# Head by head instead of with zeros: exact attention scores from stacked rounded parts, on one core

## What is computed

```
q = (xq @ Wq + bq).reshape(B, Lq, 16, 8)
k = (xk @ Wk + bk).reshape(B, Lk, 16, 8)
scores = einsum('bqhd,bkhd->bhqk', q, k) / sqrt(8)
out = einsum('bhqk,bkhd->bqhd', softmax(scores), v)
x = x + out.reshape(B, Lq, 128) @ Wo + bo
```

## Time and profile before

| | us |
|---|---|
| median of 3 runs | 1052.72 (1051.87 to 1052.78) |
| span of the profiled execution, first to last instruction | 1049.9 |
| TensorE matmuls busy | 1008.1 |
| TensorE weight loads busy | 636.9 |
| VectorE busy | 748.8 |
| GpSimd busy | 686.9 |
| ScalarE busy | 607.4 |

### The profile page before, as it was taken

One profiled execution on the slowest core, in us unless ns is written; L12 is line 12 of the kernel. 1 busy time (PEld: TensorE's weight loads), 2 busy tenths in 40 slices (PEclk: granted clock), 3 DMA queues, 4 the chain that ended last, 5 costly groups with the idle time before them and its releaser, 6 DMA issues.

```text
span 1049.9 us, 28844 instructions
## 1 busy us (share of the span) xinstructions
PE 1008.1 (96%) x11729; PEld 636.9 (61%) x11729; DVE 748.8 (71%) x1852; ACT 607.4 (58%) x898; POOL 686.9 (65%) x819
## 2 busy tenths in 40 slices
PE   7889999999999999999999999999999999999998
PEld 5345555556655776667676655665556566565576
DVE  7778888778884443776787788878888866777421
ACT  2144445577667455455554576776666677766752
POOL 6688988687986332111114699987889777688720
PEclk9699999999999999999999999999999999999999
DMA  6300000000001102000000000000000000000011
GB/s 217 122 2 2 22 12 13 20 14 23 12 22 28 36 31 99 13 7 7 8 7 19 14 8 2 2 2 2 3 1 2 2 2 2 2 2 2 1 41 41
DMA packets 9282, 22.76 MB, mean 22 GB/s; under 512 B 1392, under 2 KB 1648, under 8 KB 8768
## 3 DMA queue, kind: packets, MB, share of 16 engines
q1 hardware_dynamic: 9152, 20.94, 5.9%
HBM read 18.77 MB, written 2.15 MB: 20 GB/s over the span
## 4 chain that ended last, share of the span: by engine, by line
PE 82%; DVE 7%; POOL 5%; issue 4%; ACT 2%; DMA 0%; SPq 0%; POOLq 0%; ACTq 0%; DVEq 0%
PE weighed L708 12%; PE scores L680 11%; PE row_scores L643 7%; PE scores L906 6%; PE weighed L731 5%; PE scores L598 4%; PE quads L579 4%; DVE negmax L1226 3%; PE quads L605 3%; PE scores L693 3%; PE row_scores L906 3%; PE quads L590 3%; PE row_scores L721 2%; PE scores L721 2%; PE weighed L923 2%
## 5 line engine op out<-in xcount | busy, mean ns | idle before, releaser
L1226 DVE TENSOR_REDUCE negmax<-row_scores 128x8 f32<-128x616 f32 (+1 forms) x312 | 298.8, 958 | 100.4 <-PE row_scores L643 74.9
L1731 ACT ACTIVATE p<-scores 128x1024 f32<-128x1024 f32 (+1 forms) x253 | 250.9, 1020 | 165.6 <-PE scores L693 139.2
L680 PE MATMUL scores<-qblk,work 32*77 32x512 f32 (+1 forms) x1256 | 202.8, 612 | 6.2 <-ACT p L1731 3.3
L708 PE MATMUL weighed<-p,v 77*32 77x128 f32 (+1 forms) x5120 | 172.9, 276 | 0.1
L1906 POOL TENSOR_TENSOR qblk<-work,pack_const 128x512 f32<-128x512 f32 x160 | 166.5, 1041 | 0.0
L1916 POOL TENSOR_TENSOR kblk_r<-work,pack_const 128x308 fp32r<-128x308 f32 (+1 forms) x160 | 134.0, 838 | 44.4 <-PE row_scores L643 27.0
L643 PE MATMUL row_scores<-kblk_r,qr 32*128 32x308 f32 (+1 forms) x624 | 140.9, 443 | 13.8 <-DVE negmax L1226 12.3
L708 PEld LDWEIGHTS weighed<-p,v 77*32 77x32 f32 (+1 forms) x5120 | 130.0, 109 | 36.0 <-issue 29.4
L643 PEld LDWEIGHTS row_scores<-kblk_r,qr 32*128 32x128 f32 x624 | 61.4, 185 | 98.0 <-issue 70.9
L693 PE MATMUL scores<-nblk,select 32*77 32x512 bf16 (+1 forms) x628 | 94.8, 376 | 0.0
L1242 DVE STREAM_TRANSPOSE nat<-weighed 128x256 f32<-128x256 f32 x160 | 70.9, 443 | 32.6 <-PE weighed L708 30.7
(11 more groups left out here) (332 smaller groups left out, 1862.9 us busy)
## 6 DMA issues: line engine op xcount, KB each, us to landing
shared<-gates_hbm SPq DMA_DIRECT2D x24, 256.0 KB, 3.1
shared<-in_ctx_tok SPq DMA_DIRECT2D x15, 154.0 KB
pack_w_l<-in_w_l SPq DMA_DIRECT2D x1, 2058.5 KB, 11.5
x<-in_x_tok SPq DMA_DIRECT2D x8, 256.0 KB, 6.2
out_x<-x SPq DMA_DIRECT2D x8, 256.0 KB, 2.0
layers_w<-in_w_l SPq DMA_DIRECT2D x1, 1289.0 KB, 9.8
ctxT<-in_ctxT SPq DMA_DIRECT2D x1, 1232.0 KB, 8.9
layers_w<-in_w_ada SPq DMA_DIRECT2D x1, 582.0 KB, 5.5
```

The source lines that it names most:

```text
L680: mm = e.matmul(score_banks(n, g // 2)[0:nk, g % 2, :], k_of[q % 3][at, s * nk:(s + 1) * nk], qblk[n % 2][at, :], start=layer.mask != "qk" ...
L708: mm = e.matmul(av_bank[TILE * j:TILE * j + TILE, i2 * S:(i2 + 1) * S], v[0:nk, at:at + TILE], p[n % 2][0:nk, g * NJ + j, :], start=i1 == ...
L1226: e.tensor_reduce(negmax[q % 2][:, 2 * h:2 * h + 2, s * NJ:(s + 1) * NJ], row_banks(n, h)[:, :, 0:NJ * nk].rearrange("p g (j k) -> p g j k ...
L1731: e.activation(p[n % 2][0:nk, 8 * h:8 * h + 8, :], score_banks(n, h)[0:nk].rearrange("p g (j q) -> p (g j) q", j=NJ), ACT.Exp, bias=hide, ...
```

## The change

The exact scores no longer use fp32 matmuls and blocks with zeros. Each query and key is cut into a rounded part (fp32r) and a remainder, and their product is the sum of four products of parts, which are laid out as contraction rows: for one head, 8 dimensions times the four combinations of parts (`PARTS`) fill the 32 rows of a tile.

- The columns of the query and key weights are permuted on the host (`_by_dim`), so that inside a group of 32 partitions the row is 4 x dimension + head; the rotary tables, the shuffle and `own_head` follow.
- ScalarE rounds the keys of a quad too (`round_k`, into `k_high`), between its two exponentials at cl 3. GpSimd subtracts to get the remainders, at cl 3 (`split_q`, `split_k`, into `q_low` and `k_low`). `spread_q` and `qblk` are gone.
- SyncE stacks the parts of two sequences (a *pair*, 80 in all) with eight transfers inside SBUF, from 128 partitions into every fourth of 32 partitions with the head as an extra dimension (`stack_pair`, into `k_ring` and `q_ring`, three pairs deep). It waits for both subtractions and for the exact scores of the pair three before. Its queue is now written as a loop over slots that places gates, context tiles and pairs.
- TensorE runs 16 matmuls of 128 columns a sequence, head by head, the four row tiles in turn, and waits for the pair's transfers.
- `q_of` and `k_of` have two buffers instead of three; the freed ones hold `q_low` and `k_low`. The roundings and subtractions of a quad wait until the transfers of the quad before have landed.

```diff
+PAIRS = 3
+PARTS = [(0, 0), (0, 1), (1, 0), (1, 1)]
...
-        xn, q_of, k_of = ([work[:, 3 * i + j, :] for j in range(3)] for i in range(3))
+        xn, q_of, k_of = [work[:, j, :] for j in range(3)], [work[:, 3 + j, :] for j in range(2)], [work[:, 6 + j, :] for j in range(2)]
+        q_low, k_low = work[:, 5, :], work[:, 8, :]
+        k_high = sb("k_high", [128, QUAD * S], F32R)
...
-        qblk = [sb(f"qblk{i}", [128, NJ * S]) for i in range(2)]
+        q_ring = [sb(f"q_ring{i}", [128, NJ, 2 * S]) for i in range(PAIRS)]
+        k_ring = [sb(f"k_ring{i}", [128, NJ, 2 * S]) for i in range(PAIRS)]
...
+        def pair_landed(m):
+            return ld[f"pair{m % PAIRS}"], 16 * 2 * len(PARTS) * (m // PAIRS + 1)
...
-                w.wait_ge(qblk_done, n + 1)
-                for g in range(NG):
-                    at = slice(TILE * g, TILE * (g + 1))
-                    mm = e.matmul(score_banks(n, g // 2)[0:nk, g % 2, :], k_of[q % 3][at, s * nk:(s + 1) * nk], qblk[n % 2][at, :],
-                                  start=layer.mask != "qk" or g >= 2, stop=False, skip_group_check=True,
-                                  tile_position=(TILE * g, 0))
+                m, half = divmod(n, 2)
+                w.wait_ge(*pair_landed(m))
+                for j in range(NJ):
+                    for g in range(NG):
+                        at = slice(TILE * g, TILE * (g + 1))
+                        mm = e.matmul(score_banks(n, g // 2)[0:nk, g % 2, j * S:(j + 1) * S],
+                                      keys_of(m, nk)[at, j, half * nk:(half + 1) * nk].bitcast(F32R),
+                                      q_ring[m % PAIRS][at, j, half * S:(half + 1) * S].bitcast(F32R),
+                                      start=j == 0 and (layer.mask != "qk" or g >= 2), stop=False, skip_group_check=True,
+                                      tile_position=(TILE * g, 0))
...
+            def round_k(q):
+                cols = QUAD * layer_of(q).nk
...
+                if q:
+                    w.wait_ge(*pair_landed(2 * q - 2))
+                    w.wait_ge(*pair_landed(2 * q - 1))
+                e.copy(k_high[:, 0:cols], k_of[q % 2][:, 0:cols]).then_inc(k_rounded, 1)
...
-            def spread_q(n):
...
+            def split_q(q):
+                w.wait_ge(qr_done, q + 1)
+                if q:
+                    w.wait_ge(*pair_landed(2 * q - 2))
+                    w.wait_ge(*pair_landed(2 * q - 1))
+                e.tensor_tensor(q_low, q_of[q % 2], qr[q % 3][:, :].bitcast(F32), ALU.subtract).then_inc(q_split, 1)
...
-                    if t + 1 in jobs:
-                        spread_q(t + 1)
...
+                    if cl == 3 and qi + 2 in quads:
+                        split_q(qi + 2)
+                        split_k(qi + 2)
...
+            def stack_pair(m):
...
+                w.wait_ge(q_split, q + 1)
+                w.wait_ge(k_split, q + 1)
+                w.wait_ge(scores_done, 2 * (m - PAIRS) + 2)
+                landed = pair_landed(m)[0]
+                for x, (of_q, of_k) in enumerate(PARTS):
+                    k_src = k_low if of_k else k_high[:, :].bitcast(F32)
+                    e.dma_start(keys_of(m, nk)[x:128:NJ, :, :], k_src[:, k_at]).then_inc(landed, 16)
+                for x, (of_q, of_k) in reversed(list(enumerate(PARTS))):
+                    q_src = q_low if of_q else qr[q % 3][:, :].bitcast(F32)
+                    e.dma_start(q_ring[m % PAIRS][x:128:NJ, :, :], q_src[:, q_at]).then_inc(landed, 16)
```

More of the change, by code:

```diff
@@ L504, in build @@
         evT = attnT
-        hidden = [[work[:, k, :] for k in range(7)], [quad(normT, 2 + k) for k in range(6)] + [qblk[0][:, :]]]
+        hidden = [[work[:, k, :] for k in range(7)], [quad(normT, 2 + k) for k in range(6)] + [last_hidden[:, :]]]
         gate_z = four(1, 1)
         gate_sig = [rot[0][:, :] if c == NB - 1 else four(1, 2 + c % 2) for c in range(NB)]
-        mix_in = [qblk[1][:, 0:NE * D], four(1, 0)[:, 0:NE * D]]
+        mix_in = [first_mix[:, :], four(1, 0)[:, 0:NE * D]]
         mix_step = nat
```

115 lines of the change are left out of this document (73 added, 42 removed).

## The result

The changed kernel takes 1065.18 us (median; 1063.28 to 1066.44 over 4 runs) beside 1052.75 us (1051.87 to 1053.03) for the one before: a ratio of 1.012, with an interval from 1.0106 to 1.0135. It is 1.2% slower; 1004 us had been forecast. The profiled execution took 1066.09 us, its span is 1063.9.

What follows compares the result with a forecast made beforehand. TensorE, busy for 96% of the span, was taken as the bound. 49.6 us saved by stage, less 1 for ScalarE, took 48.6 off 1049.9, giving 1001.3 of span; with 2.8 added, 1004 us, range 976 to 1044.

Steps and rivals of the forecast that it cites:

- What TensorE loses and gains: Exact scores on TensorE: 16 tiled pairs cost 0.55 or 0.60 us instead of 0.93 or 0.96, saving 59.5 of queue.
- (2): Rival, chance 0.07: 128-column matmuls on TensorE take four passes, so the distance stays 0.93 us and the time 1045 to 1055.
- (4): Rival, chance 0.06: weight-load and matmul pairs on TensorE do not run side by side; 16 take 2.2 us, the kernel 1250.
- From TensorE's queue to time, by stage: Per-quad saving left after VectorE's share: l0 1.2, l0c and l2 1.3 each, l3s 0.9, l3c 1.5 us; 49.6 in all.
- GpSimd: GpSimd loses 166 us of query spreads and gains 75 of subtractions; the net 91 beside TensorE is worth nothing by itself.
- ScalarE: ScalarE gains one key rounding a quad, about 22 us of work, costing 1 us over 24 narrow quads.
- SyncE and the transfers: SyncE issues a pair's eight transfers in 5.2 us, 2.0 from issue to landing, within two slots of about 7.0.
- The cover of 0.9 us: Slack between the landing of a quad's last transfers and ScalarE's key rounding, 0.9 us, the thinnest cover of the change.
- rival (1): Chance 0.13: narrow fourth slots wait for a landing or GpSimd, giving part of the saving back; 20 us saved, 1033.
- (3): Rival, chance 0.12: transfers become the bound if one costs over 0.96 us; about 1140 at 1.2 each, 1067 at 1.0.
- high end: Top of the predicted time range: rival (1) and the unhidden loads together, about 1042, taken as 1044 us.
- the unhidden loads: TensorE's weight loads not hidden: 16 pairs cost 0.82 or 0.99 us, 0.11 saved with 77 keys, nothing with 128.

Runs made afterwards that it cites:

- e10: Changed kernel with rounding and subtraction in halves, and narrow slots' second row scores issued mid-weighing: 1017.03 us, ratio 0.9664 to the kernel before.
- e9: Changed kernel with rounding and subtraction split in two halves of a quad, each waiting for one earlier pair only: 1057.66 us, ratio 1.0057 to the kernel before.
- e1: Changed kernel with the stacking transfers of the first three pairs only and the exponential's scale lowered: 1057.47 us, ratio 1.0076 to the kernel before.
- e2: Changed kernel with all transfers, but exact scores as four fp32 matmuls of 512 columns, as long as before: 1056.45 us, ratio 1.0040 to the kernel before.
- e5: Changed kernel with fourteen full matmuls of constants before the first exact scores of phase 1: 1073.93 us, ratio 1.0206 to the kernel before.
- e11: Changed kernel with narrow slots' second row scores issued mid-weighing and no transfers after the first three pairs: 1029.24 us, ratio 0.9785 to the kernel before.
- e12: e10 with one full matmul of constants before the exact scores of phase 0's first and last twelve sequences: 1021.53 us, ratio 0.9726 to the kernel before.
- e6: Changed kernel with full matmuls of constants before exact scores, fourteen at phase 1's start, two at each remaining sequence: 1095.37 us, ratio 1.0415 to the kernel before.

## Why the prediction was wrong

**What TensorE loses and gains.** Right in kind and too careful: 0.33 us for the sixteen pairs against a forecast of 0.55. They run side by side over the four tiles at 21 ns a pair, and four rounds of 128 columns in 0.33 us leave no room for four passes (1.0 us at 0.49 ns a column), so rivals (2) and (4) are out. The nearest row, the weighing at 32 ns a pair, was the right one to go by. The 81 ns of the Trainium skill (TensorE: Matmul & The Clock Gate, "Back-to-back issue gap") would have missed by four times for tiled pairs.

**From TensorE's queue to time, by stage.** This step failed. I looked at each stage for the busy time of the runner-up, found VectorE at 10.12 of 15.27 us in l3c, and let all 1.5 us a quad through. Measured at full clock: about 0.3 us a quad in l0 for 1.2, nothing in the middle quads of l0c and l2 for 1.3, 0.3 in l3s for 0.9, nothing in l3c for 1.5; 8 us in all for 49.6. Busy time does not show a loop that passes through one buffer. Between the two sets of row scores lie 1.40 us, of which 1.25 are the row scores' start and VectorE's 0.80, whatever stands between. The numbers were in the trace of before: 881.41 and 882.80 for the two sets, with the exact scores at 881.41 to 882.34 between them. The saving fell exactly into that gap. The step was applied with care only in l3s, where the wait was already visible. In e10, with the order mended, the forecasts by stage hold wherever the clock is full: l3c 13.5 to 14.4 for 13.8, l0c and l2 13.5 to 14.4 for 14.0 to 14.3, l3s 16.2 to 17.1 for 16.4; only l0, at 20.5 for 19.7, gains almost nothing. (l3s has these lengths in the change as well.)

**GpSimd.** The net saving was 70 us (686.9 to 617.2), not 91: subtractions take 1.27 and 0.84 us where I had taken 1.04 and 0.70 from spreads. Operations on two full tiles took 1.27 us before as well (`x<-x,gated`); the spreads have a small second operand. Whether the subtractions cost time is not shown by a run of their own. TensorE's weight loads wait 34.4 us for key spreads where it was 16.4, but in e10, with all subtractions, it is 16.9 again.

**ScalarE.** The rounding of 308 columns takes 0.44 us, for 0.5 taken. What I costed at 1 us for the whole kernel was its work; its wait was the cost.

**SyncE and the transfers.** Issue at 0.60 to 0.65 us each, 5.1 us a pair, and 2.0 to 2.1 us to landing are as forecast. The cover of 0.9 us was the step that failed here, as rival (1) had it: waits of up to 2.3 and 2.8 us, 12.2 and 7.7 us in all, instead of under 0.3 each. I counted it for one pair from the release of its ring slot. The loop is that of the quad: sixteen issues, landing, rounding, subtraction, all through one buffer of remainders, 15 to 17 us against a quad that was to become 13.8. With that sum made beforehand the forecast would have been at best 15.1 a quad in l3c, no gain. Halves end it, as e9 and e10 show.

**Not in the sum at all: the clock.** Neither the forecast nor a rival had that TensorE's stalls would be followed by 15 to 40 us at 1.2 GHz. The change's mean clock is 0.949 against 0.990. In two quads at the start of phase 1 alone this cost 7.4 and 2.4 us, and in all quads touched by it 22 us. Only part of this follows from waits for landings: without them (e1, e9) the mean clock of the profiled executions is 0.963 and 0.955.

**Which rival came in.** Rival (1) came in for its part, late landings, 7.5 us by e9. What kept the saving from coming out, the loop of the row maxima, and what made the change slower, the clock, are in no rival. (3) would have needed 0.96 us a transfer and the usual issue takes 0.60 to 0.65. The time lies above the range, because 8 us of saving came out at full clock, where (1) left 20, and the quads with half clock took 22. The range was also summed wrongly: its high end, said to be (1) and the unhidden loads together, takes 10.6 us off 1052.7 for the loads and leaves out the 29 us that (1) gives back. With them it is 1071, and 1065 would have lain inside it by luck, without either of the two mechanisms.

## What to carry to other kernels

Before a saving on the bounding engine is counted, follow each buffer with a single copy around its loop and write down the period: writer, reader, and what now fills the time between. If the removed work stood in that time, it was free. Where a feeding loop (here issue, landing, rounding, subtraction) is within a few per cent of the present period, shortening the main path makes it the bound; mend both in one step, and do not judge either edit by itself. And look at the granted clock before reading the stages of a kernel whose bounding engine has less to do: a quad at 1.2 GHz hides what an edit did at 2.4.

## What the hardware showed that was not expected

- 640 transfers take the queue from 9152 packets and 20.94 MB to 101312 and 94.84, and with all their roundings and subtractions cost 4 us while the exact scores are long (e2). There ScalarE and GpSimd still waited 6.8 and 5.9 us for landings.
- In the change and its variants the granted clock fell after standstills that are short: 1.71 us on TensorE at 606 to 608 us (the change), 2.18 us at 641.7 (e5), 0.93 us at 712 (e9); it then stayed at 0.50 for some 15 to 40 us, in the change with TensorE busy for 34.49 of 35 us. A standstill does not suffice: e2 had 1.93 us at 607 and stayed at 1.00. The kernel before, with 2.11 and 1.42 us of standstill at 41 and 46 us, was back at full clock by 55 us, e10 with the same standstills only between 70 and 80.
- It also fell without one: in e10 at 295 us, after five microseconds with TensorE busy for 4.68 and no standstill over 0.32. e11 and e12 have a fall at the same place (0.68 and 0.67 at 295 to 300 us), and the change and e1 one at 300 to 305 (0.50). Windows of e10:

```profile
290.00:295.00 5.00, 4.68 (x102) 2.77 (x91) 4.78 (x14) 4.55 (x8) 4.05 (x7) 0.94 0.56 184
295.00:300.00 5.00, 5.00 (x50) 3.59 (x47) 1.77 (x5) 2.41 (x5) 2.76 (x5) 0.50 0.38 114
```

With long exact scores (e2) or two full matmuls a sequence (e6) there was no fall at this place, and behind 100 us only one short dip each (0.66 in a window of 5 us). That less or thinner work on TensorE exposes the clock is shown; what exactly brings a fall is left open.
